# A transformer chain on one core: last Newton products crossed over the array, both factor sets loaded at the start, a new table of places

## What is computed

```python
for _ in range(6):
    KV = K @ V
    V = 0.25 * V @ (13*I - KV @ (15*I - KV @ (7*I - KV)))
SV = (kernel1 @ V) @ (kernel3 @ values)
```

## Time and profile before

| what | value |
|---|---|
| device time, 3 runs | 2515.51 us median (2512.83 to 2518.18) |
| profiled execution, its own device time | 2522.18 us |
| its span | 2520.2 us, 95538 instructions |
| TensorE products busy | 2266.3 us (90%) |
| VectorE busy | 1956.9 us (78%) |
| ScalarE busy | 1450.1 us (58%) |
| GpSimd busy | 387.1 us (15%) |
| mean granted TensorE clock | 0.953 |

### The profile page before, as it was taken

How to read it: one execution, slowest core, us unless ns; L and a number is a source line. 1 busy time by engine, 2 the same in 40 slices (tenths; PEclk the granted TensorE clock), 3 DMA queues, 4 the chain that set the end, 5 groups by cost and what they waited for, 6 DMA issues and landing times.

```text
span 2520.2 us, 95538 instructions
## 1 busy us (share of the span) xinstructions
PE 2266.3 (90%) x40576; PEld 1846.1 (73%) x40576; DVE 1956.9 (78%) x6166; ACT 1450.1 (58%) x5093; POOL 387.1 (15%) x530
## 2 busy tenths in 40 slices
...
DMA packets 29960, 35.75 MB, mean 14 GB/s; under 512 B 3544, under 2 KB 28128, under 8 KB 28384
## 3 DMA queue, kind: packets, MB, share of 16 engines
...
## 4 chain that ended last, share of the span: by engine, by line
PE 52%; DVE 28%; ACT 15%; issue 4%; POOL 0%; DMA 0%; SPq 0%; POOLq 0%; DVEq 0%; ACTq 0%
PE ps L477 29%; PE ps L480 8%; ACT probs L1062 5%; PE ps L744 4%; DVE probsT L1349 3%; PE ps L828 3%; ACT probs L1047 3%; PE ps L876 2%; ACT ey L985 2%; DVE x_rows L1211 2%; DVE small L1252 2%; PE ps L761 2%; PE ps L665 2%; DVE qk_v L1337 1%; DVE p L1254 1%
## 5 line engine op out<-in xcount | busy, mean ns | idle before, releaser
L1102 POOL TENSOR_TENSOR small<-small,weights 128x1 f32<-128x1 f32 x256 | 149.0, 582 | 1142.7 <-DVE small L1200 1142.7
L1010 ACT ACTIVATE probs<-ps,small 128x128 f32<-128x128 f32 x1024 | 286.1, 384 | 31.0 <-DVE small L1342 29.5
L1349 DVE COPY probsT<-ps 128x512 f32<-128x512 f32 x384 | 263.1, 685 | 36.3 <-PE ps L480 32.7
L480 PE MATMUL ps<-weights,probs 128*128 128x128 f32 x1536 | 256.1, 292 | 32.8 <-ACT probs L1010 15.4
L1342 DVE TENSOR_REDUCE small<-ps 128x4 f32<-128x512 f32 x384 | 254.2, 683 | 20.5 <-PE ps L828 10.7
L1113 POOL TENSOR_TENSOR probs<-probs,small 128x256 f32<-128x256 f32 x128 | 108.7, 849 | 885.6 <-DVE small L1478 885.6
L480 PEld LDWEIGHTS ps<-weights,probs 128*128 128x128 f32 x1536 | 178.7, 146 | 86.3 <-ACT probs L1010 44.6
L929 ACT COPY x_T<-ps 128x128 f32<-128x128 f32 x128 | 34.1, 267 | 302.9 <-PE ps L480 302.9
L1062 ACT ACTIVATE probs<-ps,small 128x128 f32<-128x128 f32 x512 | 181.6, 375 | 20.5 <-DVE small L1342 19.0
L477 PE MATMUL ps<-wz,ss 64*64 64x72 f32 x6144 | 157.4, 229 | 32.5 <-DVE wz L1294 32.4
L1293 DVE SCALAR_TENSOR_TENSOR wz<-ey,ss 128x256 f32<-128x256 f32 x320 | 142.0, 444 | 51.1 <-ACT ss L970 36.9
...
## 6 DMA issues: line engine op xcount, KB each, us to landing
...
```

What stands on the lines that cost most here:

```text
L480: return nc.tensor.transpose(dst, src, ident)
L1010: ins = nc.scalar.activation(probs(s, g)[:, j], bank(s, SCORE_BANK[g], 128 * j, 128), ACT.Exp, bias=sm(s, "nb", 4 * g + j, 1), scale=-1.0)
L1102: nc.gpsimd.tensor_tensor(sm(s, out), sm(s, ve), w("mhalf"), ALU.pow).then_inc(sem(done, s), 1)
L1349: V.tensor_copy(probsT(s, n % 4).rearrange("p a b -> p (a b)"), bank(s, 2)).then_inc(sem("pT", s), 1)
```

## The change

1. **W5 and n.w cross.** Their 16 products each go to output half `m ^ g`, bank `g`, in the order of the other crossed steps. In exchange VectorE takes the crossed group g = 1 of W5 in two operations of 64 partitions instead of one of 128, and its `n.w` in four operations of 4 pairs instead of two of 8 pairs.
2. **n.kk is one step.** The 16 products alternate between the row halves and wait for the later `n.e1T` copy, with one semaphore at the end.
3. **Both factor sets at the start.** Two large buffers (`fc_large0`, `fc_large1`; together they take the place of `fc_A`, `fc_B`), and the small factors lie in buffers of stream 0 that are still free (`probs`, `probsT`; `k_alone_q8_o8_`). The fc2 loads follow directly behind the weights; SyncE's later wait and loads are gone. The small factors are loaded in two halves and scaled in four operations each (`scale0`, `scale1`). F1 is composed in 32 products of 256 columns.
4. **The first n.proj** waits for x transposed and the first weights only; the rows of x have a semaphore of their own, for which the first `n.out` waits on VectorE.
5. **A new table.** PERIOD goes from 74.45336 to 74.44163, and all places are new.

```diff
-            for c in range(2):
-                pe.wait_ge(sem("n_eT", s), at("n_eT", s, 3 + c))
-                for i in range(4):
+            pe.wait_ge(sem("n_eT", s), at("n_eT", s, 4))
+            for i in range(4):
+                for c in range(2):
                     for m in halves:
                         t = k2T[M * c:M * c + M, i, m]
                         mm = one(PS[s][m, 1 - c, M * i:M * i + M], t, t)
-                mm.then_inc(sem("n_first_ps", s), 1)
-                yield f"n.kk{c}"
+            mm.then_inc(sem("n_first_ps", s), 1)
+            yield "n.kk"
...
-                            mm = one(PS[s][halves[m if last else m ^ g], g, PW * i + a:PW * i + PW], ss[halves[m], p, 0:M],
+                            mm = one(PS[s][halves[m ^ g], g, PW * i + a:PW * i + PW], ss[halves[m], p, 0:M],
...
-            for h in range(H):
-                _, _, p, m = heads(h)
-                mm = one(PS[s][m, 0, 16 * p:16 * p + HD], p2[m, p], ey[m, p, M:PW])
+            for i in range(4):
+                for g in range(2):
+                    p = 4 * g + i
+                    for m in range(2):
+                        mm = one(PS[s][halves[m ^ g], g, 16 * i:16 * i + HD], p2[halves[m], p], ey[halves[m], p, M:PW])
...
-                        ins = V.scalar_tensor_tensor(Y, src[:, :, M:PW], 0.25, uy[:, ps], ALU.mult, ALU.add)
+                        for to, at_ps in ((slice(0, 128),) * 2,) if g == 0 else zip(halves, halves[::-1]):
+                            ins = V.scalar_tensor_tensor(Y[to], src[at_ps, :, M:PW], 0.25, uy[to, ps], ALU.mult, ALU.add)
...
-            for m, half in enumerate(halves):
-                ins = V.tensor_tensor(w9[half, :, m, 0:HD], v[half], sm(s, "rd")[half].unsqueeze(2).to_broadcast([M, PAIRS, HD]),
-                                      ALU.mult)
+            for g in range(2):
+                v = bank(s, g, 0, 64).rearrange("p (a b) -> p a b", b=16)[:, :, 0:HD]
+                for m, half in enumerate(halves):
+                    ins = V.tensor_tensor(w9[half, 4 * g:4 * g + 4, m, 0:HD], v[halves[m ^ g]],
+                                          sm(s, "rd", 4 * g, 4)[half].unsqueeze(2).to_broadcast([M, 4, HD]), ALU.mult)
...
-            yield "load"
-            sp.wait_ge(once("composed"), 1)
             factor_loads(1)
-            yield "factors"
+            yield "load"
...
             for c in range(16):
-                mm = mmul(PS[1][:, 0], small[:, c], big[:, c], start=(c == 0), stop=(c == 15))
+                for half in range(2):
+                    f = slice(256 * half, 256 * half + 256)
+                    mm = mmul(PS[1][:, 0, f], small[c // 8][:, c % 8], big[:, c, f], start=(c == 0 and half == 0), stop=(c == 15),
+                              skip_group_check=True)
...
-                if n == 1:
-                    pool.wait_ge(once("composed"), 1)
-                small = mixed[n][0]
-                nc.gpsimd.tensor_tensor(small, small, over(mix_col[:, n], D), ALU.mult).then_inc(once("scaled"), 1)
+                for q in range(4):
+                    part_of = mixed[n][0][q // 2][:, 4 * (q % 2):4 * (q % 2) + 4]
+                    nc.gpsimd.tensor_tensor(part_of, part_of, over(mix_col[:, n, 4 * q:4 * q + 4], D), ALU.mult
+                                            ).then_inc(once("scaled"), 1)
```

More of the change, by code:

```diff
@@ L64 @@
 BATCHES = B
-PERIOD = 74.45336
+PERIOD = 74.44163
 PLACES = {
     "sp": (
-        "n.xT 2.607  n.x 72.513  ",
+        "n.xT 3.082  n.x 72.988  ",
         "r1.ctxT 83.425  r1.ctx 83.485  rf.ln 233.799  ",
@@ L72 @@
     "pe": (
[16 rows of a table removed]
[16 rows of a table added]
     ),
     "act": (
[11 rows of a table removed]
[11 rows of a table added]
     ),
     "pool": (
[L104 to L107, removed]
+        "n.lm0 -10.045  n.lm1 -1.243  n.out 56.683  ",
+        "r1.ctx 86.992  r1.out 121.357  rm.out 123.440  r2.xbo 139.964  r2.out 152.459  ry.stats 159.179  "
+        "ry.xbo 171.964  ry.p0 172.887  ry.p1 186.993  ry.p2 196.999  ry.p3 197.703  ry.out 209.055  "
+        "rf.out 223.061  ",
     ),
     "dve": (
[17 rows of a table removed]
[17 rows of a table added]
     ),
@@ L132 @@
     "sp": (
-        "load -1000.0000  factors 62.1304  "
+        "load -1000.0000  "
     ),
     "pe": (
[6 rows of a table removed]
[8 rows of a table added]
     ),
@@ L146 @@
     "pool": (
-        "scale0 36.0000  prepare 40.0000  scale1 60.0000  "
+        "scale0 -1.2330  prepare -1.2230  scale1 -1.2130  "
     ),
     "dve": (
-        "clear -1000.0000  mix -999.0000  col -998.0000  f1 63.6294  f2 145.7884  "
+        "clear -1000.0000  mix -999.0000  col -998.0000  f1 79.1600  f2 138.8530  "
     ),
@@ L279, in build @@
         with ExitStack() as factors:
-            fa = sb("fc_A", [128, 8192], scope=factors)
-            fb = sb("fc_B", [128, 2048], scope=factors)
+            fa = [sb(f"fc_large{n}", [128, 8192], scope=factors) for n in range(2)]
         of_lane.append(lane_buffers(1))
@@ L310, in body @@
     (orow, z, zT, res, PS, sm, over, every) = (o[k] for k in "orow z zT res PS sm over every".split())
-    wpack, rows, b2, a1, b1, a2, b2w, fa, fb, mix, mix_col, mix_tmp, left = (
-        o[k] for k in "wpack rows b2 a1 b1 a2 b2w fa fb mix mix_col mix_tmp left".split())
-    mixed = [(fb[:].rearrange("p (c d) -> p c d", c=16), a1, fa[:].rearrange("p (c f) -> p c f", c=16), b1),
-             (fb[:].rearrange("p (c d) -> p c d", c=16), b2w, fa[:].rearrange("p (c f) -> p c f", c=16), a2)]
+    wpack, rows, b2, a1, b1, a2, b2w, fa, mix, mix_col, mix_tmp, left = (
+        o[k] for k in "wpack rows b2 a1 b1 a2 b2w fa mix mix_col mix_tmp left".split())
+    small_at = [(pp[0], pT[0]), (ka[0][:, 0:8], ka[0][:, 8:16])]
+    mixed = [(a, b, fa[n][:].rearrange("p (c f) -> p c f", c=16), d) for n, (a, b, d) in
+             enumerate(((small_at[0], a1, b1), (small_at[1], b2w, a2)))]
     def once(name):
@@ L428, in start @@
                              ).then_inc(once("mix_in"), 16)
-            sp.dma_start(xin[:], x[0]).then_inc(once("first_in"), 16)
+            sp.dma_start(xin[:], x[0]).then_inc(once("rows_in"), 16)
             factor_loads(0)
@@ L437, in start @@
             sp.dma_start(b2s[0:EXPERTS], b2).then_inc(once("weights_in"), 16)
+            factor_loads(1)
             yield "load"
-            sp.wait_ge(once("composed"), 1)
-            factor_loads(1)
-            yield "factors"
         def factor_loads(n):
             small, small_src, big, big_src = mixed[n]
-            sp.dma_start(small, small_src).then_inc(once("small_in"), 16)
             for half in range(2):
                 c = slice(8 * half, 8 * half + 8)
-                sp.dma_start(big[:, c], big_src[:, c]).then_inc(once("factor_in"), 16)
+                sp.dma_start(small[half][:], small_src[:, c]).then_inc(once(f"small{n}_in"), 16)
+            for half in range(2):
+                c = slice(8 * half, 8 * half + 8)
+                sp.dma_start(big[:, c], big_src[:, c]).then_inc(once(f"large{n}_in"), 16)
         def rest(s):
@@ L498, in nystrom @@
             else:
-                pe.wait_ge(once("first_in"), 16 * 3)
+                pe.wait_ge(once("first_in"), 16 * 2)
             one(bank(s, 0, 0, 128), w("n_q"), xTin[:]).then_inc(sem("proj", s), 1)
@@ L897, in start @@
             small, _, big, _ = mixed[0]
-            pe.wait_ge(once("scaled"), 1)
-            pe.wait_ge(once("factor_in"), 16 * 2)
+            pe.wait_ge(once("scaled"), 4)
+            pe.wait_ge(once("large0_in"), 16 * 2)
             for c in range(16):
-                mm = mmul(PS[1][:, 0], small[:, c], big[:, c], start=(c == 0), stop=(c == 15))
-                if c == 15:
-                    mm.then_inc(once("composed"), 1)
-                yield f"f1.{c}"
-            pe.wait_ge(once("scaled"), 2)
-            pe.wait_ge(once("factor_in"), 16 * 4)
+                for half in range(2):
+                    f = slice(256 * half, 256 * half + 256)
+                    mm = mmul(PS[1][:, 0, f], small[c // 8][:, c % 8], big[:, c, f], start=(c == 0 and half == 0), stop=(c == 15),
+                              skip_group_check=True)
+                    if c == 15 and half == 1:
+                        mm.then_inc(once("composed"), 1)
+                    yield f"f1.{2 * c + half}"
+            small, _, big, _ = mixed[1]
+            pe.wait_ge(once("scaled"), 8)
+            pe.wait_ge(once("large1_in"), 16 * 2)
             for f in range(4):
                 for c in range(16):
-                    mm = mmul(PS[1][:, 1, 128 * f:128 * f + 128], big[:, c, 128 * f:128 * f + 128], small[:, c],
+                    mm = mmul(PS[1][:, 1, 128 * f:128 * f + 128], big[:, c, 128 * f:128 * f + 128], small[c // 8][:, c % 8],
                               start=(c == 0), stop=(c == 15))
@@ L1157, in scale @@
                 pool.wait_ge(once("mix_col"), 1)
-                pool.wait_ge(once("small_in"), 16 * (n + 1))
-                if n == 1:
```

(8 more changed lines are left out.)

9 lines of the change are left out of this document (5 added, 4 removed), and 102 rows, old and new, of tables (PLACES, START).

## The result

The changed kernel is slower: 2593.99 us, median of 4 runs (2580.16 to 2601.23), against 2515.08 (2512.83 to 2518.18). The ratio is 1.0306, 95% interval [1.0262, 1.0351]. The profiled execution took 2580.16 us with a span of 2578.4. It is the fastest of the four (granted clock 0.960; the others had 0.947 to 0.951 and took 13 to 21 us more), while the profiled execution before is above the median of its kernel.

A forecast was written before the change was run, and what follows sets the result against it. PE, 93% busy, nearly fills the period, with the serial Nyström chain as long. 36 us from thirty batches at 1.2 plus 10 from the start gave 46: from 2515.5 to 2469 us, range 2443 to 2503 (8 in 10).

The forecast's parts named there:

- The order "even": Steady state: the new order saves about 0.5 us from W5 to `n.o`; earlier S2 and longer S2 to W2 cancel.
- Rival C: S2 to W2: ACT's `ry.e1` ahead of `n.S21` delays W2; period 1.4 us longer, 2547 us, or 2530; chance 0.12.
- Saved work is saved time: Steady period: PE loses 1.18 us of work and, being 93% busy, the period loses 1.2 us; 36 us over thirty batches.
- Rival A: Steady period: PE's saved time turns idle, only the chain's 0.3 us is left; 18 us in all, 2497; chance 0.20.
- W5 to `n.o`: End of a batch: from 3.56 us to 3.03 in the new order, 0.5 less.
- W5, n.w, n.kk: PE's steps: W5 and `n.w` go from 1.03 us to 0.66 each, `n.kk` from 1.10 to 0.66.
- rival D: W5 and `n.w`: crossing does nothing for eight columns, by the bank rule or another; 2518 us; chance 0.06.
- `n.kk` on the chain: `n.kk` starts 0.54 us later, for the second `e1T` copy, and takes 0.44 less: +0.10, counted as nothing.
- DVE's `n.w`: Four operations of half the size instead of two: 0.75 us instead of 0.46, +0.29 on the chain.
- The start: First two batches: 6 us less in the first, 4 in the second; 10 us in all, between 3 and 16.
- `scale1`: First batch: moving it up removes a 2.9 us wait; its four quarters hold up DVE 0 to 3.6 us, taken as 2.
- The clock: Half-clock spells cost some 1.1 us each; a rival had fewer spells, 17 us more gain, 2452 us; chance 0.10.

The follow-up runs named there:

- e1: The changed kernel's code and start, with every engine's steady order from the table of before: 2516.45 us, ratio 0.9984 to the kernel before.
- e17: The change's code in the old steady order, with W1 to W2 alone in the new order on PE, DVE and ACT: 2561.97 us.
- e3: The changed kernel with `ry.e1` moved behind `n.S21` and `r1.z` on ACT, and `n.S21` moved up behind `n.S20` on DVE: 2664.17 us, ratio 1.0575.
- e6: The changed kernel with W1 to W2 put back to the old order on PE, DVE and ACT: 2572.83 us, one execution.

## Why the prediction was wrong

**The order "even".** This is the step that failed. The prediction priced only the steps around the last products, at half a microsecond of gain, and called the rest even ("I call these two even"), while the table reorders all lists. The period was to lose 1.2 us and grew by 2.30, of which the order makes all. In windows at full clock the loss of 2.46 us divides, by putting back, into W1 to W2 1.00 (75.10 to 74.10), the `r2.t3` swap 0.88 (74.27 to 73.39), the end 0.31 (73.39 to 73.08), the rest of the order 0.29 (to 72.79), and the code in the old order 0.15 (72.79 against 72.64); the stretch `n.e3T0` to `n.kk` without the swap goes the other way by 0.17. The shares depend on what else is in place: put into e1 alone, the swap costs 1.04 and W1 to W2 1.63; and in the new order the code gains 0.13 (75.23 to 75.10) instead of costing 0.15. In the means of the same runs, one execution each, W1 to W2 gives 0.26, the swap 0.71 and the end 1.11. The "rest" of 0.29 was not taken apart. The swap was in no term and in no rival, nor among the stretches shown above as those that differ most.

**Rival C** named the right stretch and the right mechanism: the copy for S21 stands behind `ry.e1`, and DVE's S21 comes 1.54 later behind S2 (4.21 instead of 2.67). S2 to W2 grew by 1.45 in the window shown, near its 1.5, and by 1.83 in the one of the table. But it was given 0.12, and its count, "W2 comes 0.1 to 0.7 later", was too low. S2 did come sooner behind W1 (2.50 to 2.86 instead of 3.00), which pays a part of it; counted from `n.proj` it came later, at 39.65 to 40.02 instead of 39.07, for W0 was already 1.08 late. And the stretch is only 1.00 of the 2.46: C left out the rest of the order. Whether `ry.e1` makes all of the stretch's loss stays open: no run moves it alone.

**Saved work is saved time** failed as well. The work itself was forecast right: 1.18 us less of PE per period, 1.2 measured at full clock with the code in the old order. Rival A (0.3 per period) is the nearest to what the code alone did, and even its 0.3 was not there: the code in the old order gives -0.15 per window at full clock, the crossing alone 0.12 (72.64 to 72.52). In the old order DVE's `rm.out` stands ahead of Y5; in the new one it stands behind, W5 to `n.o` is 0.29 shorter than before, and the period is longer all the same.

**W5, n.w, n.kk** at 0.66: measured 0.58 (814.69 to 815.27), 0.58 and, in e1, 0.62 (1579.51 to 1580.13). Right, rival D is out. The rule that different row tiles cannot use one PSUM bank at once (the Trainium skill, TensorEngine Tiling (Array Packing), Gotcha 1) costs nothing that is seen here: both halves write one bank, and the 16 products take 0.58. The uncrossed form wrote one bank from both halves too, and took 1.03, so the bank didn't tell the two apart; whether two products wrote it at the same moment the rows don't show. `n.kk` on the chain: +0.10 forecast and counted as nothing, +0.20 measured. DVE's `n.w`: 0.75 forecast, 0.79 measured. W5 to `n.o`: 3.03 forecast, 3.27 measured; W5 to `n.w` is 1.45 (905.41 to 906.86) where 1.16 was counted, with DVE's three operations at 0.61 instead of 0.45.

**The start** was right in sum, and partly by luck. Second and third `n.proj` were forecast at 76 and at 152 to 153; the timeline of PE after:

```profile
74.94 1.19 PE L479 MATMUL ps<-x_in_T,weights 128*128 128x128 f32 x4 [0.45 <-ACT x_firstT L937]
...
153.12 1.19 PE L479 MATMUL ps<-x_in_T,weights 128*128 128x128 f32 x4 [0.50 <-ACT x_firstT L937]
```

That is 7.5 and 9.8 us earlier than the earlier trace rows. The first batch gained more than its 6, the second 2.3 instead of 4. Within the first, `n.S0` starts 6.4 earlier (34.00 instead of 40.41; forecast 5.5 and some tenths), S0 to W5 is 0.1 shorter (forecast 0.9), and W5 to `n.proj` 1.0 shorter where 0.6 longer was counted. Three of the four quarters of `scale1` still hold DVE once, for 2.2 us in all (forecast 2); the longest two are 1.04 and 1.02 for operations of 0.18, under one row of GpSimd:

```profile
46.03 4.37 POOL L1169 TENSOR_TENSOR k_alone_q_o<-k_alone_q_o,mix_col 128x512 f32<-128x512 f32 x4
```

```profile
46.08 1.04 DVE L1303 TENSOR_TENSOR u<-ss,ey 128x32 f32<-128x32 f32 x1
...
47.37 1.02 DVE L1302 SCALAR_TENSOR_TENSOR wz<-ey,ss 128x32 f32<-128x32 f32 x1
```

**The clock.** The scatter was named; a gain of it was a rival of its own, and a loss stood in C as one more spell. Mean less shortest window is 1.17 before, 1.01 after, 1.14 in e17 and 2.3 in e3, so in the profiled executions it explains none of the change's own loss, but it decides what a cure of one stretch is worth (e6). It may be part of the 21 us that the medians differ by beyond the profiles: the three executions without a profile had the lower granted clock. No trace shows their windows.
